# Attention values scaled a pair at a time by one multiplication and summed over heads by two reductions a sequence

## The reference

```
xn = (input - mu) * rsqrt(var + EPS) * gamma + beta         # one mu, var a sequence
q = Wq @ xn + bq;  k, v = split(Wkv @ context + bkv)        # (16, 8*64, 256)
att = softmax((q*s) . (k*s), axis=-1)                       # s = 64 ** -0.25, per head 256 x 256
y = att . v                                                 # per head 256 x 64
out = Wo.T @ y.reshape(n, 8*64, 256) + bo
return input + out
```

## Time and profile before

| | |
|---|---|
| median of 3 runs | 228.07 us (227.21 to 231.05) |
| the profiled execution, span | 228.2 us |
| TensorE busy | 208.6 us, 91% |
| VectorE busy | 199.3 us, 87%, 589 instructions |
| ScalarE busy | 181.1 us, 79% |
| GpSimd busy | 160.3 us, 70% |
| mean granted TensorE clock | 0.965 |

### The profile page before, as it was taken

The page is one execution under the profiler, slowest core; times in us unless marked ns, Lnnn a source line. Parts: engine busy times, 40 slices in busy tenths (PEclk is TensorE's granted clock), DMA queues, the critical chain, the costliest instruction groups (busy, mean ns, idle before and its releaser), DMA issues.

```text
span 228.2 us, 7194 instructions
## 1 busy us (share of the span) xinstructions
PE 208.6 (91%) x2511; PEld 179.9 (79%) x2511; DVE 199.3 (87%) x589; ACT 181.1 (79%) x371; POOL 160.3 (70%) x157
## 2 busy tenths in 40 slices
PE   6968878799999999999999998999999999999872
PEld 6857757588888798889888887888888888887761
DVE  3589987879898999899999999999999998989765
ACT  2374586787889988898889888989897979888880
POOL 5135185777987877789788887789686869776460
PEclk9975897999999999999999999999999999999998
DMA  5964137480767566566665665656657656442000
GB/s 134 261 272 93 27 82 174 107 184 14 164 141 160 131 153 142 132 141 151 140 153 122 160 151 121 151 127 154 142 127 166 149 133 143 93 94 62 13 3 23
DMA packets 31090, 29.04 MB, mean 127 GB/s; under 512 B 4240, under 2 KB 29840, under 8 KB 31056
## 3 DMA queue, kind: packets, MB, share of 16 engines
q1 hardware_dynamic: 30224, 28.07, 52.4%
q10 hardware_dynamic: 832, 0.53, 1.0%
HBM read 3.80 MB, written 1.05 MB: 21 GB/s over the span
## 4 chain that ended last, share of the span: by engine, by line
PE 41%; POOL 20%; issue 13%; ACT 11%; DVE 11%; ACTq 2%; POOLq 0%; DVEq 0%
POOL p_lo L773 19%; PE ps_sc L522 6%; PE ps_max L546 6%; PE ps_sc L523 5%; PE ps_z L479 4%; ACT p_full L678 4%; DVE neg_max L894 4%; ACT p_hi L675 3%; PE ps_z L481 3%; PE ps_z L480 3%; PE ps_z L414 3%; PE ps_m L589 2%; PE ps_t L497 2%; PE ps_m L590 2%; DVE z_sum L910 2%
## 5 line engine op out<-in xcount | busy, mean ns | idle before, releaser
L773 POOL TENSOR_TENSOR p_lo<-p_full,p_hi 128x512 f16<-128x512 f32 x122 | 139.9, 1163 | 42.3 <-ACT p_full L678 41.2
L675 ACT ACTIVATE p_hi<-ps_sc 128x512 f16<-128x512 f32 x128 | 77.9, 608 | 18.3 <-PE ps_sc L523 15.9
L894 DVE TENSOR_REDUCE neg_max<-ps_max 128x2 f32<-128x512 f32 x128 | 85.9, 677 | 6.9 <-PE ps_max L546 6.8
L678 ACT ACTIVATE p_full<-ps_sc 128x512 f32<-128x512 f32 x128 | 78.7, 615 | 0.0
L522 PE MATMUL ps_sc<-t_a,c_seq 128*128 128x256 f32 x256 | 71.2, 300 | 3.5 <-issue 2.6
L523 PE MATMUL ps_sc<-t_b,c_seq 65*128 65x256 f32 x256 | 67.3, 284 | 0.0
L479 PEld LDWEIGHTS ps_z<-u_hi,p_hi 128*128 128x128 f16 x512 | 46.4, 97 | 12.8 <-issue 8.2
L479 PE MATMUL ps_z<-u_hi,p_hi 128*128 128x65 f16 x512 | 53.0, 195 | 2.2 <-DVE p_lo L930 1.9
L522 PEld LDWEIGHTS ps_sc<-t_a,c_seq 128*128 128x128 f32 x256 | 49.2, 192 | 5.9 <-issue 4.6
L480 PE MATMUL ps_z<-u_lo,p_hi 128*128 128x64 f16 x512 | 52.8, 193 | 0.0
L481 PE MATMUL ps_z<-u_hi,p_lo 128*128 128x65 f16 x512 | 52.7, 194 | 0.0
(11 more groups left out here) (108 smaller groups left out, 233.9 us busy)
## 6 DMA issues: line engine op xcount, KB each, us to landing
t_a<-t_a SPq DMA_DIRECT2D x90, 128.0 KB, 2.4
t_b<-t_b SPq DMA_DIRECT2D x30, 128.0 KB, 2.5
x_seq<-x_hi SPq DMA_DIRECT2D x15, 128.0 KB, 2.4
c_pad<-c_hi SPq DMA_DIRECT2D x30, 64.0 KB, 2.1
c_seq<-c_hi SPq DMA_DIRECT2D x15, 128.0 KB, 2.4
x_res<-x_tiles SPq DMA_DIRECT2D x4, 256.0 KB, 6.7
out<-x_res SPq DMA_DIRECT2D x16, 64.0 KB, 2.0
x_seq<-x_lo SPq DMA_DIRECT2D x15, 64.0 KB, 2.1
```

Source lines behind the costliest of these rows:

```text
L675: nc.scalar.activation(p_hi[:, buf, :, :].rearrange("p t s -> p (t s)"), scores, ACT.Exp).then_inc(act_phi, 1)
L678: nc.scalar.activation(p_full[:, head % 2, :], scores, ACT.Exp).then_inc(act_p, 1)
L773: nc.gpsimd.tensor_tensor(p_lo[:, buf, :, :].rearrange("p t s -> p (t s)"), p_full[:, head % 2, :], p_hi[:, buf, :, :].rearrange("p t s -> ...
L894: nc.vector.tensor_reduce(to, ps_max[:, unit % 2, :].rearrange("p (t s) -> p t s", t=KT), X, ALU.max, negate=True).then_inc(dve_max, 1)
```

## The change

At an even step, VectorE now reduces the step's maxima first. Then it waits for TensorE's pair, takes the reciprocals, waits for them, and multiplies all 4 x 64 values of the pair by their reciprocals (the reciprocal is read with a step of zero over 64 columns) in one TENSOR_TENSOR of 256 columns, into a new SBUF buffer `z_parts`. That buffer holds four heads (two pairs) and a fifth slot. At the odd step after the second pair (h7) one TENSOR_REDUCE adds the four heads, 512 elements a partition, into the fifth slot. At the odd step after the fourth pair (h3) a second one adds the next four heads and the fifth slot, 640 elements, into `z_sum`. The reduction is over the head index, which is outermost in memory: its innermost read steps 128 fp32 words (512 bytes). The reduction is issued after the step's maxima and before `u_lo` (L924) of the same step. TensorE's permission to refill a `ps_z` bank now comes from the multiplication. The columns of a pair in `ps_z` are ordered by head and then by query tile.

```diff
+        z_parts = sb("z_parts", [P, H // 2 + 1, KT, C], fp32)
...
+        def sum_at(n, h):
+            e = av_at(*divmod(n * H + h - 1, H))
+            return (e[0], e[1] // 4) if e and e[1] % 4 == 2 else None
...
-                    need(pe, dve_zsum, (m * PAIRS + first // 2 - 1) * 2 * KT)
+                    need(pe, dve_zpart, m * PAIRS + first // 2 - 1)
...
-                            z0 = (qt * 2 + head % 2) * Z_W
+                            z0 = (head % 2 * KT + qt) * Z_W
...
-                    pe.wait_ge(dve_zsum, (m + 1) * H * KT)
+                    pe.wait_ge(dve_zsum, 2 * (m + 1))
...
+            def scale_values(m, first):
+                pair = first // 2
+                sums = ps_z[:, pair % 2, 0:4 * Z_W].rearrange("p (k t z) -> p k t z", t=KT, k=2)
+                inv = inv_sum[:, pair % 2, :].rearrange("p (k t z) -> p k t z", t=KT, k=2)
+                dve.wait_ge(pe_av, m * H + first + 2)
+                nc.vector.reciprocal(inv, sums[:, :, :, C:C + 1]).then_inc(dve_inv, 1)
+                dve.wait_ge(dve_inv, m * PAIRS + pair + 1)
+                if pair % 2 == 0:
+                    need(dve, dve_zsum, m * 2 + pair // 2)
+                nc.vector.tensor_tensor(z_parts[:, first % 4:first % 4 + 2], sums[:, :, :, 0:C], inv.broadcast_to([P, 2, KT, C]),
+                                        ALU.mult).then_inc(dve_zpart, 1)
+
+            def add_values(m, part):
+                dve.wait_ge(dve_zpart, m * PAIRS + 2 * (part + 1))
+                if part == 0:
+                    total, count = z_parts[:, H // 2], H // 2
+                    need(dve, dve_zsum, 2 * m)
+                else:
+                    total, count = z_sum[:, m % 2], H // 2 + 1
+                    dve.wait_ge(dve_zsum, 2 * m + 1)
+                    need(dve, pe_y, m - 1)
+                nc.vector.tensor_reduce(total, z_parts[:, 0:count].rearrange("p h t c -> p t c h"), X, ALU.add).then_inc(dve_zsum, 1)
...
-                z_step = av_at(n, h)
-                if z_step:
-                    m, first = z_step
-                    pair = first // 2
...
-                    dve.wait_ge(pe_av, m * H + first + 2)
-                    nc.vector.reciprocal(inv, sums[:, :, :, C:C + 1]).then_inc(dve_inv, 1)
-
                 for m, unit in max_at(n, h):
                     dve.wait_ge(pe_s1, m * H + unit + 1)
...
-                if z_step:
...
-                            if head == 0:
-                                nc.vector.tensor_scalar(total, part, scale, 0.0, ALU.mult, ALU.add).then_inc(dve_zsum, 1)
-                            else:
-                                dve.wait_ge(dve_zsum, (m * H + head - 1) * KT + qt + 1)
-                                nc.vector.scalar_tensor_tensor(out=total, in0=part, scalar=scale, in1=total, op0=ALU.mult,
-                                                               op1=ALU.add).then_inc(dve_zsum, 1)
+                if e := sum_at(n, h):
+                    add_values(*e)
+                if e := av_at(n, h):
+                    scale_values(*e)
```

More of the change, by code:

```diff
@@ L32 @@
 T_EARLY = 6
-T_AHEAD, T_LO_AHEAD, MAX_AHEAD, AV_BEHIND = 12, 11, 11, 4
-UP_AHEAD, TB_AHEAD, DUP_AHEAD = 11, 10, 7
+T_AHEAD = 12
+T_LO_AHEAD = 11
+MAX_AHEAD = 11
+AV_BEHIND = 4
+UP_AHEAD = 11
+TB_AHEAD = 10
+DUP_AHEAD = 7
 P_BUFS = 8
@@ L185, in xattn_program @@
         act_thi, act_phi, act_p = sem("act_thi"), sem("act_phi"), sem("act_p")
-        dve_tlo, dve_max, dve_inv, dve_zsum = sem("dve_tlo"), sem("dve_max"), sem("dve_inv"), sem("dve_zsum")
+        dve_tlo, dve_max, dve_inv = sem("dve_tlo"), sem("dve_max"), sem("dve_inv")
+        dve_zpart, dve_zsum = sem("dve_zpart"), sem("dve_zsum")
         dve_ulo, dve_y = sem("dve_ulo"), sem("dve_y")
@@ L879, in step @@
                                             ALU.subtract).then_inc(dve_tlo, 1)
-                z_step = av_at(n, h)
-                if z_step:
-                    m, first = z_step
-                    pair = first // 2
-                    sums = ps_z[:, pair % 2, 0:4 * Z_W].rearrange("p (t k z) -> p t k z", t=KT, k=2)
-                    inv = inv_sum[:, pair % 2, :].rearrange("p (t k z) -> p t k z", t=KT, k=2)
-                    dve.wait_ge(pe_av, m * H + first + 2)
-                    nc.vector.reciprocal(inv, sums[:, :, :, C:C + 1]).then_inc(dve_inv, 1)
                 for m, unit in max_at(n, h):
```

## The result

The changed kernel takes 234.85 us (median of 4 runs, 233.5 to 235.7). The ratio to the kernel before is 1.028, with a 95% interval of 1.0215 to 1.035. I had forecast 225.8 and a range of 223.5 to 234.0. With a fourth run, the median of the kernel before is 228.25 us. The profiled execution has a span of 233.6 us and took 235.4. The metric is thus 1.8 us above the span, which I had overlooked when I set the old span of 228.2 beside the old median. The difference of the two spans is 5.4 us.

The account below looks back on a forecast made before the run. VectorE and TensorE bound the kernel as one loop, where the place of VectorE's work counts. From 228.2 us, 13 sequences 0.20 shorter (2.6 less) and 0.3 more at the end gave 225.8; range 223.5 to 234.0.

Parts of the forecast that it names:

- the price of the two reductions: VectorE at h7 and h3: contiguous rate despite the 512-byte step, 0.60 and 0.73 us by starts, 1.33 together.
- rule of adjacent pairs: Skill's rule for VectorE reads: full rate only for elements in adjacent pairs, else 1.73 ns a column; estimate 233.
- the walk: Costs carried along VectorE's order through one sequence, with TensorE's times; claimed the sequence shortens by 0.20 us.
- rival 1: Stepped read in both reductions is slow; at two turns an element a sequence grows 0.75 us, total 238.9; chance 0.27.
- Multiplication by starts 0.34: Even step on VectorE: the 256-column multiplication takes 0.34 us by starts, between bounds 0.33 and 0.39.
- Reciprocal to multiplication 0.20: Even step on VectorE: reciprocal is followed at once by its reader, so its uncovered latency costs 0.20 us.
- The first reduction hidden up to a length of 0.85: Before `u_lo` of h7: idle 0.48 us and shortened steps hide the 512-element reduction up to 0.85 us.
- The waits of TensorE at h3: TensorE's waits for the maxima of h1 and L917 go: 0.15 us, up to 0.30 in the timeline's sequence.
- what is late next: TensorE's transposition L458 behind the maxima of h4: a round trip that stays; before, 0.39 us a sequence.
- 13 x 0.20: Steady part, about 50 to 205 us: 13 sequences each 0.20 us shorter, 2.6 us less.
- the sum: Whole kernel: 228.2 - 2.6 + 0.3 gives 225.8 us; the tail's share is 0.26 more.
- 1.7 turns: Stepped read in the reductions at 1.7 turns an element: 234 us; half of the slow-read chance lies below it.

Follow-up runs that it names:

- Experiments 1: Changed kernel, both reductions adding 4 or 5 words side by side instead of 512 bytes apart (wrong elements summed): 228.42 us, ratio 1.001.
- experiment 5: Changed kernel with z_parts in rows of 6 words, heads innermost, sums right (the kernel in rows of six): 227.62 us, ratio 0.992.
- experiment 4: Changed kernel plus VectorE reductions and multiplications run one by one behind its last step, to price each alone: one run, 249.3 us.
- experiment 3: Changed kernel with the wait for the pair and the reciprocal back ahead of the maxima, reductions still stepped: 230.19 us, ratio 1.004.

## Why the prediction was wrong

**The step that failed** is the price of the two reductions, "Bounds: 1.04 ns an element from below ... and 1.04 + 3.8 from above. I take the lower." Measured, an element read with the step costs (1.00 - 0.07) us / 512 = 1.8 ns by starts, 1.75 turns of 1.04 ns (0.07 is what 512 x 1.04 ns leave of the 0.60 us of a contiguous reduction). The sum of the two reductions is 2.24 us a sequence instead of 1.33. Experiments 1 and 5 remove the step alone and get the forecast lengths, 0.68 and 0.81.

**Why I took the lower.** I leaned on L811, which ended 0.03 us behind GpSimd. That row could not decide. It has 32 elements, for which even the surcharge now measured is 32 x 0.75 ns = 0.02 us. Its step is 3 words, too, which no run measured, and experiment 4 shows that the price depends on the step: none at 2 words, the full price at 4. Then I took one sentence of the Trainium skill against another. The Trainium skill, "Vector Engine (DVE) Microarchitecture Reference", section 5.2, has 1.73 ns a column for one source that hops at every element, and the trace comes close (1.8 ns). Its rule of adjacent pairs, which the prediction repeats, does not hold here for a step of 2 words (0.69 us, the full rate). The same section's one-source operation at the full rate looked more like the reduction, since it writes less than it reads. Here it does not carry over: 512 into 128 with a step of 128 words costs as much (1.02 us) as 512 into one with a step of 4 (1.05 us).

**The mechanism and the walk were right.** Put 1.75 turns into the prediction's walk: the reductions take 1.00 and 1.23, `u_lo` of h7 starts at 166.07, the second half takes 6.77, and the maxima of h4 come at 172.84, a sequence of 12.09 us. Measured: 12.08. With the forecast prices the walk gave 11.44, and experiments 1 and 5 have 11.41 and 11.42. With only the first stepped it gives 11.59 (measured 11.58), with only the second 11.95 (11.93). That is rival 1, to which I had given 0.27.

**The other terms.** Multiplication by starts 0.34, as taken. Reciprocal to multiplication 0.20, as taken; its 0.44 a sequence is shown by experiment 3. The first reduction hidden up to a length of 0.85: at 0.60 it is (experiment 5), at 1.00 it is late by 0.17, where the walk has 0.15. The waits of TensorE at h3 go, and what is late next is the transposition behind the maxima of h4, as said; its wait grew to 0.99. The multiplication is 0.42 us long beside GpSimd's work and alone, so nothing stretches it. "13 x 0.20" was 2.5 us in 12 sequences of the kernel in rows of six. The earlier return of the `ps_z` banks, which ends a wait of TensorE that the prediction did not price, was not tested by itself. For the changed kernel the 12 sequences lost 3.4, not 12 x 0.43 = 5.2, because the five longest (12.0 to 12.8 us before) lost 0.3 or less each. The walk does not cover those.

The end of the kernel fits the sum in one view and not in another. From TensorE's last pair to the last transposition TensorE idles 1.26 us before, and in experiment 5 and after:

```profile
221.24 0.33 PE L569 MATMUL ps_m<-ident,z_sum 128*128 128x128 f32 x1 [1.59 <-DVE z_sum L830]
...
230.58 0.48 PE L569 MATMUL ps_m<-ident,z_sum 128*128 128x128 f32 x1 [2.00 <-DVE z_sum L830]
```

That is 0.33 more with the forecast's prices, against 0.26 in the sum, and 0.74 more with the stepped reductions. But from the thirteenth output step to the last it takes 20.88 us before, 21.49 in experiment 5 and 22.55 after, so 0.6 and 1.7 more. Where the rest of that comes from was not followed.

**The range.** It ended at 234.0, where the prediction put 1.7 turns. At 1.75 turns its sum gives 228.2 + 13 x 0.45 + 0.76 = 234.8, which is the measured time and lies just outside. That this sum meets the 234.85 so closely is in part luck: it puts more on the sequences than the 3.4 us that they lost, and less on the end. Given a figure of 1.65 turns for a source that hops at every element, and a row too short to contradict it, the slow read should have been the likelier case, and the forecast near the 233 that the prediction worked out for it.

## What to carry to other kernels

Count VectorE's work by starts and not by durations, and then ask in which stretch it lies. Here 0.40 us more ahead of a wait cost 0.17 a sequence, and 0.51 in the stretch without slack cost 0.52. An instruction that reads what the one before it made should have another one between, worth 0.11 us at each place here. That is more than all that one multiplication for four additions leaves once the reductions are paid at the full rate (0.76 - 0.34 = 0.42 us a pair, less 1.33 / 4 = 0.33). Before a rearranged view goes into an operation, look which of its dimensions is innermost in memory: a rearranged layout of the buffer, with the step put on the PSUM side, gave the same sums at the full rate.

## What the runs showed of the hardware

- VectorE reading fp32 from SBUF: 512 elements with a step of 1 or 2 words take 0.68 to 0.69 us, with 4 or 8 words 1.05, with 32 or 128 words 1.02. The free step of 2 was unexpected: in that view no two consecutive elements are neighbours.
- The same step of 128 words from PSUM costs nothing (0.69 us). Two heads read 130 words apart in PSUM cost the multiplication nothing (0.42 us).
- Writing every word 6 words behind the last takes the 256-column multiplication from 0.42 to 0.60 us alone and 0.635 beside other work. An output of one word per four read, 6 words apart, costs nothing (0.69 us, the last reduction into rows of six in experiment 4).
- The number of outputs does not matter: 512 into 128 and 512 into 1 take 0.68 and 0.69 us.
